# A graph-attention layer on one core: five of the 128 adjacency loads issued in two pieces, of 120 and of 8 partitions

## The reference

```
h = relu(layernorm(x)) @ W                              # 8192 x 128
e = leaky_relu(s_src[:, None] + s_dst[None, :], 0.2)    # s_src = h @ a[:128], s_dst = h @ a[128:]
e = where(adj > 0, e, -9e15)                            # adj: 8192 x 8192 int32, one entry in 2048 is 1
out = x + softmax(e, axis=1) @ h
```

## Time and profile before

| | |
|---|---|
| time, median of 3 runs | 805.73 us (805.66 to 805.8) |
| profiled execution, its own time | 804.8 us |
| its span, first to last instruction | 803.0 us |
| busy: PE / DVE / ACT / POOL | 64% / 76% / 66% / 64% of the span |
| adjacency loads, one each | 2048 KB, median 18.7 us from issue to landing |

### The profile page before, as it was taken

One profiled execution on the slowest core, in us unless ns is written; L12 is line 12 of the kernel. 1 busy time (PEld: TensorE's weight loads), 2 busy tenths in 40 slices (PEclk: granted clock), 3 DMA queues, 4 the chain that ended last, 5 costly groups with the idle time before them and its releaser, 6 DMA issues.

```text
span 803.0 us, 9015 instructions
## 1 busy us (share of the span) xinstructions
PE 515.2 (64%) x1855; PEld 229.5 (29%) x1855; DVE 606.7 (76%) x3167; ACT 526.8 (66%) x371; POOL 512.5 (64%) x522
## 2 busy tenths in 40 slices
PE   3778666766577576666667676676767676656521
PEld 3652222322222232322222222222222232222221
DVE  7956678667776768777779778777786798888984
ACT  3879667676767767766767767676666767676300
POOL 4753776656666665577767666656777756775671
PEclk9888656676855766777666767667666556676655
DMA  8999999999999999999999999999999999999310
GB/s 334 423 386 390 406 403 406 409 411 407 408 408 409 409 407 401 406 398 393 380 406 397 405 396 399 392 408 397 400 389 398 389 399 399 389 380 402 120 37 15
DMA packets 40903, 299.31 MB, mean 373 GB/s; under 512 B 11052, under 2 KB 14034, under 8 KB 24464
## 3 DMA queue, kind: packets, MB, share of 16 engines
q1 hardware_dynamic: 22976, 276.83, 85.3%
q0 software_dynamic: 15328, 17.58, 6.9%
q10 hardware_dynamic: 2544, 4.33, 1.6%
HBM read 304.31 MB, written 8.65 MB: 390 GB/s over the span
## 4 chain that ended last, share of the span: by engine, by line
DMA 68%; DVE 10%; ACT 10%; issue 8%; PE 3%; POOLq 0%; ACTq 0%; DVEq 0%
DMA adj_buf<-in_adj 67%; ACT mask_buf L467 9%; DVE x_all L820 3%; PE banks L1048 2%; DVE stats L559 2%; PE banks L1017 1%; DVE mv_all L563 1%; DMA x_all<-in_x 1%; PE banks L1007 0%; DVE newton L576 0%; DVE rstd L580 0%; DVE newton L578 0%; PE banks L1089 0%; DVE mask_buf L589 0%; ACT work L431 0%
## 5 line engine op out<-in xcount | busy, mean ns | idle before, releaser
L467 ACT ACTIVATE mask_buf<-adj_buf,minus_half 128x2048 bf16<-128x2048 int32 x252 | 493.0, 1994 | 205.9 <-DMA adj_buf<-in_adj 205.4
L361 POOL DMA_INDIRECT gathered<-table,index x448 | 448.5, 1001 | 242.5 <-issue 145.9
L1048 PE MATMUL banks<-mask_buf,bit_ident 128*128 128x512 bf16 x1024 | 388.5, 527 | 99.8 <-ACT mask_buf L467 99.0
L1048 PEld LDWEIGHTS banks<-mask_buf,bit_ident 128*128 128x128 bf16 x1024 | 107.9, 124 | 325.7 <-ACT mask_buf L467 187.7
L820 DVE SCALAR_TENSOR_TENSOR x_all<-gathered,weight,x_all 128x128 f32<-128x128 f32 x512 | 157.7, 348 | 7.2
L635 DVE MAX8 words<-banks 128x8 f32<-128x512 f32 x64 | 44.7, 698 | 119.9 <-PE banks L1048 119.8
L1046 PE MATMUL banks<-key_rows,ones_b 3*128 3x512 bf16 x64 | 31.7, 495 | 119.2 <-ACT mask_buf L467 118.8
L1089 PE MATMUL banks<-x_all,one_hot 128*128 128x128 f32 x128 | 44.0, 445 | 18.3 <-DVE x_all L820 18.3
L1046 PEld LDWEIGHTS banks<-key_rows,ones_b 3*128 3x128 bf16 x64 | 6.1, 95 | 147.8 <-ACT mask_buf L467 145.9
L639 DVE MAX8 words<-rest 128x8 f32<-128x512 f32 x64 | 44.5, 695 | 2.2
L1089 PEld LDWEIGHTS banks<-x_all,one_hot 128*128 128x128 f32 x128 | 36.1, 317 | 27.5 <-DVE x_all L820 19.5
(11 more groups left out here) (162 smaller groups left out, 537.9 us busy)
## 6 DMA issues: line engine op xcount, KB each, us to landing
adj_buf<-in_adj SPq DMA_DIRECT2D x128, 2048.0 KB, 18.7
gathered<-table,index POOLq DMA_INDIRECT x448, 6.4
table<-gathered ACTq DMA_DIRECT2D x4, 1040.0 KB, 14.7
x_all<-in_x SPq DMA_DIRECT2D x3, 1024.0 KB, 10.8
out<-x_all SPq DMA_DIRECT2D x2, 1280.0 KB, 23.0
x_all<-in_x SPq DMA_DIRECT2D x2, 512.0 KB, 5.3
out<-x_all SPq DMA_DIRECT2D x1, 1024.0 KB, 25.5
w_gathered<-table,w_index POOLq DMA_INDIRECT x24, 5.3
```

What stands on the lines that cost most here:

```text
L361: nc.gpsimd.indirect_dma_start(g_cols[buf][:, k, :], None, table, bass.IndirectOffsetOnAxis(index[:, buf, k:k + 1], 0), bounds_check=N, oo ...
L467: nc.scalar.activation(mask_buf[:, u], adj_buf[:, u], ACT.Sign, bias=minus_half[:]).then_inc(mask_ready, 1)
L1048: ins = mm(bank, bit_ident[:, h * PART_BITS + c], mask_buf[:, u, c * BIT_COLS:(c + 1) * BIT_COLS], start=False, stop=(h == PARTS - 1 and c ...
```

## The change

Five loads are named by batch and quarter: (6, 0), (11, 2), (17, 0), (22, 2), (28, 0). Numbered through, these are loads 24, 46, 68, 90 and 112 of 0 to 127. For each of them SyncE issues a DMA of partitions 0 to 119 and, right behind it, a DMA of partitions 120 to 127, both with the same semaphore, each raising it by 16. The bytes and their places are the same. The consumers' counts go through `landed(i, u)`, which adds 16 for each such load on the quarter up to batch i, so they wait for both pieces. The other 123 loads are as before.

```diff
+LIGHT = 120
+LIGHT_LOADS = ((6, 0), (11, 2), (17, 0), (22, 2), (28, 0))
...
+        def landed(i, u):
+
+            return 16 * (i + 1 + sum(1 for j, k in LIGHT_LOADS if k == u // 2 and j <= i))
...
             def load_two(i, u):
                 source = rows_of(adj, i * BATCH + u // PARTS, 1)[:, 0, u % PARTS * PART:(u % PARTS + 2) * PART]
-                sp.dma_start(adj_buf[:, u:u + 2, :].rearrange("p u n -> p (u n)"), source).then_inc(adj_loaded[u // 2], 16)
+                place = adj_buf[:, u:u + 2, :].rearrange("p u n -> p (u n)")
+                if (i, u // 2) in LIGHT_LOADS:
+                    sp.dma_start(place[0:LIGHT], source[0:LIGHT]).then_inc(adj_loaded[u // 2], 16)
+                    sp.dma_start(place[LIGHT:], source[LIGHT:]).then_inc(adj_loaded[u // 2], 16)
+                else:
+                    sp.dma_start(place, source).then_inc(adj_loaded[u // 2], 16)
...
-                act.wait_ge(adj_loaded[u // 2], 16 * (i + 1))
+                act.wait_ge(adj_loaded[u // 2], landed(i, u))
...
-                    dve.wait_ge(adj_loaded[u // 2], 16)
+                    dve.wait_ge(adj_loaded[u // 2], landed(0, u))
```

## The result

The changed kernel takes 872.34 us (median of 4 runs, 871.95 to 874.73) against 805.69 us: a ratio of 1.0834, 95% interval 1.0814 to 1.0854. It is 66.6 us slower, 13.3 us for each of the five loads, where 15 us less were forecast.

The account below looks back on a forecast made before the run. One lagging DMA engine was taken to pace the adjacency loads. Ending the other engines' pauses after 334 us (9.8 us) and less lag at the last load (5.5 us) sum to 15.3 us: 789.5 us from 804.8, range 783 to 800.

Parts of the forecast that it names:

- What bounds the kernel: Adjacency loads: one of sixteen DMA engines lags, about 8.5 us behind at the end, and every load lands with it.
- 21.6 us of slack: Over the adjacency stream, the laggard's lag against the other fifteen engines: 120 loads x 0.18 us.
- The dealing: In the five split loads, 120 rows go as 15 engines x 8 rows, the other 8 as 8 engines x 1.
- Which engine is relieved: In the five loads the last engine is left out; if it is the laggard, relief is 24.5 to 25.7 us.
- the sign that the prediction named for this: Before the last load's masks: a stretch with 8 large packets, with rate 396 GB/s, means the laggard was not relieved.
- the first rival: The laggard is another engine: 805.7 us if it keeps 8 rows, 808.9 if it takes a ninth; chance 0.09.
- the one left out is the laggard: Main forecast for the five loads: the engine without a part is the laggard, 15.3 us gained; chance 0.84.
- The Trainium skill's remark on DMA engines 7 and 15: These DMA engines are usually slower; engine 7 as laggard would give 808.9 us, engine 15 the forecast.
- A row costs 4.9 / 8 = 0.61 us: Time of one 16 KB adjacency row on a DMA engine, from the fast stretch; 0.64 us by the queue's share.
- what it adds to an engine is one row: Reason to charge nothing for the second piece of each of the five loads, with three loads queued around it.
- the bad bound: Second pieces of the five loads exposed from issue to landing: 5 x 1.8 = 9 us.
- The 805.7 us that the prediction set beside its forecast: By the skill's rules for kernel authors, transfers of disjoint partitions gain nothing, so the time stays 805.7 us.

Follow-up runs that it names:

- Experiment 7: Kernel before plus one extra DMA of k rows, memory to unused memory, after each of batches 1 to 31: 804.48 us (k=2), 806.14 (3), 824.73 (4), 822.09 (7).
- experiment 1: Changed kernel with the same five loads cut into two pieces by columns (128 partitions x 2048 columns each) instead of by partitions: 805.47 us, ratio 0.9998 to the kernel before.
- (3): Changed kernel with the five loads cut into pieces of 64 and 64 partitions instead of 120 and 8: 864.55 us, ratio 1.0723 to the kernel before.
- experiment 5: Changed kernel, five loads loading only half their rows, as four DMAs of 16 partitions: into partitions 32 to 95 792.3 us, into 0 to 63 808.4 us.
- (6): Changed kernel with the five loads as eight DMAs of 16 partitions, alternating between lower and upper half of the partitions: 834.49 us, ratio 1.035 to the kernel before.
- (4): Changed kernel, same pieces of 120 and 8, but read from 2 MB lying in one block of memory: 873.63 us, ratio 1.085 to the kernel before.
- (2): Changed kernel with only the piece of 120 partitions, the piece of 8 and its count left out: 863.36 us, ratio 1.071 to the kernel before.

## Why the prediction was wrong

**What bounds the kernel: right.** One DMA engine lands every load last and the others are ahead of it. Experiment 7 shows it: three engines could take 19 us more for nothing, near the 21.6 us of slack that the rates gave, and the fourth could take none.

**The dealing: right.** 15 and 8 engines, by the packet counts.

**Which engine is relieved: wrong.** By the dealing rule the change leaves out the sixteenth, and the laggard is the fourth. The trace of the changed kernel has the sign that the prediction named for this: its last masks start at 814.67 us, and in 805.5 to 810.5 us there are again only 8 packets of 8 KB or more, one of them an instruction packet.

```profile
DMA packets 969, 2.04 MB, mean 408 GB/s; under 512 B 24, under 2 KB 27, under 8 KB 961
```

The fourth takes a ninth row in each of the five loads. This is the first rival, given 0.09, and by itself it would have made 3.2 us, 808.9 us. The forecast of 0.84 for "the one left out is the laggard" rested on no row; the trace had named none. The Trainium skill's remark on DMA engines 7 and 15 (page "DMA: Bandwidth & Descriptors", section "Latency and other measured facts") did not hold here. Numbered from 0, as the prediction took them, these are the eighth and the sixteenth, and the laggard is among the first four.

**The step that failed** by size is the cost of the pieces: "A row costs 4.9 / 8 = 0.61 us", used for a transfer of any shape, and "what it adds to an engine is one row", with 9 us as the bad bound. Rows of the full loads were taken as the price of rows in a shape that no row of the trace showed. Measured, the piece of 120 costs 58 us and the piece of 8 another 8.5 us, where the sum had nothing for either. The 8.5 us come near the bad bound of 9 us by chance: the bound was for the exposed time from issue to landing, and a second piece with its issue and its semaphore cost nothing in experiment 1. The mechanism has no counterpart in the prediction: work was counted by DMA engine alone, and the side of the buffer that the rows go to was not counted at all. The 805.7 us that the prediction set beside its forecast, for transfers of disjoint partitions, missed this cost too: two halves took 864.55 us (3).

What takes its place, as far as shown: the time of a row depends on which partitions are written together (experiments 5 and 6), not on the number of pieces (1), the equality of the shares (3) or the memory rows (4). With 128 partitions the 16 KB rows take 0.65 us on all engines at once. With 120 they take 1.32 us over the slow stretch, for as long as the load and parts of its neighbours are moved. The Trainium skill, page "SBUF — State Buffer", section "Door 1: The DMA port swizzle", gives the picture: sixteen ports with eight partitions each, partitions p and p + 32 on the same one, partitions 0 to 63 on only eight of them. The trace agrees: sixteen engines on partitions that this rule puts on sixteen ports take 0.65 us a row, on eight ports 1.18. If 120 partitions are dealt eight in a row to each engine, then engines four apart have the same ports in the same order and write to one port as long as they go in step; that dealing in a row is inferred from the doubled time and was not seen. By the same rule the eight rows of the second piece lie on two ports, four on each; it fits that in the middle of the slow stretch, 166 to 170 us, 0.51 MB, 31 rows, take 88.7% of 16 x 4 us, 1.8 us each:

```profile
DMA packets 85, 0.54 MB, mean 134 GB/s; under 512 B 34, under 2 KB 46, under 8 KB 54
...
q1 hardware_dynamic: 43, 0.51, 88.7%
```

So by these numbers the change would have been slower even with the right engine left out, though no run shows it: it relieves some 24.5 us, at a price of 58.

**Not settled.** A load whose rows take double time should cost 4.9 us more, half a load 2.45. Half a load costs 3.2 (experiment 5), but a whole one 11.8 (3) and 11.6 (2), and 5.9 in the alternating order (6). The slow stretch of 19 us moves nearly two loads' bytes at half rate, so the neighbouring loads are slowed too; how engines in one load hold up those in the next was not taken apart. Why the fourth engine lags stays open as well: its 21.6 us come near the 23 us of instruction fetches in the stream, but the run meant to test it added none. Nor was a kernel tried that relieves the fourth engine. By the dealing rule a DMA on this queue leaves it out only if it goes over the first three engines or fewer, and three would carry 16/3 of what is taken from every engine: with 21.6 us of slack, some 4 us at best by an estimate from these numbers, before any collision on the ports.

## What to carry to other kernels

A DMA has two sides of parallel parts, the engines that move it and the places it goes to; a count of rows per engine is only the first. Before a transfer is cut by partitions, take the new shape as unmeasured and bound it by at least double the time of a row (here 1.32 us for 0.65, and the neighbouring loads lost time too), or cut it by columns, which was free here. And if one engine is suspected, find out which: a small extra DMA over the first k engines, with k raised by one, names it in a few runs. Count the packets of each such run: the one with a single row went over sixteen engines.

## What the runs showed of the hardware that was not expected

The busy share of the DMA engines does not show that they are held up: it was 1.02 at 200 GB/s. In these runs a full share with a fallen rate (200, 222, 233, 240 and 306 GB/s) went with the partitions that the rows were written to. One of sixteen engines fell behind the others on equal work, by the prediction's estimate 0.18 us in 5.66 us a load, or 3%; that the first three could take 19 us more over the 120 loads, 0.16 us each, bears this out. It was the fourth. And the order in which equal rows are written, halves in turn or one half after the other, changed the cost of a load from 11.8 to 5.9 us.
